# Depthwise taps on VectorE: the even tile of each pair runs one tap ahead of the odd one

## What is computed

```python
# x: (8, 256, 32, 32)
x = x + conv(layernorm_over_channels(x))
#   conv: qkv = 1x1 conv to 768 channels
#         agg = depthwise 5x5 conv of qkv (padding 2), then a grouped 1x1 conv
#         ms  = concat(qkv, agg);  per head of 24 channels: q, k = relu, v with a column of ones
#         out = q @ (k^T @ v);  out[..., :-1] / (out[..., -1:] + 1e-15)
#         out = 1x1 projection to 256 channels, then batchnorm
t = tokens(x)
t = t + ffn(layernorm(t))
#   ffn: softmax over 11 partitions from the image's mean token, top 2, weights of 6 experts;
#        gelu(t @ W1 + b1) per expert (341 wide), @ W2 + b2, weighted sum
x = from_tokens(t)
```

## Time and profile before

| what | value |
|---|---|
| median of 3 runs | 1441.13 us (1438.97 to 1443.95) |
| profiled execution | 1441.29 us, span 1439.6 us |
| PE busy | 1352.3 us (94%) |
| DVE busy | 1225.3 us (85%) |
| ACT busy | 1061.3 us (74%) |
| POOL busy | 977.9 us (68%) |
| mean granted clock of PE | 0.987 |

### The profile page before, as it was taken

The page is one execution under the profiler, slowest core; times in us unless marked ns, Lnnn a source line. Parts: engine busy times, 40 slices in busy tenths (PEclk is TensorE's granted clock), DMA queues, the critical chain, the costliest instruction groups (busy, mean ns, idle before and its releaser), DMA issues. The chain is left out here.

```text
span 1439.6 us, 18715 instructions
## 1 busy us (share of the span) xinstructions
PE 1352.3 (94%) x6844; PEld 771.3 (54%) x6844; DVE 1225.3 (85%) x1276; ACT 1061.3 (74%) x1890; POOL 977.9 (68%) x741
## 2 busy tenths in 40 slices
...
DMA packets 14251, 32.75 MB, mean 23 GB/s; under 512 B 2384, under 2 KB 5328, under 8 KB 13904
## 3 DMA queue, kind: packets, MB, share of 16 engines
...
## 5 line engine op out<-in xcount | busy, mean ns | idle before, releaser
L1154 DVE SCALAR_TENSOR_TENSOR dacc<-qkvs,dww,dacc 128x960 f32<-128x960 f32 (+4 forms) x930 | 1026.8, 1187 | 0.0
L1001 POOL TENSOR_TENSOR gl<-hb,gh 128x512 f16<-128x512 f32 x256 | 307.0, 1206 | 212.3 <-ACT hb L752 210.0
L962 POOL TENSOR_TENSOR dwo<-dwo,tapb 128x992 f32<-128x992 f32 (+2 forms) x100 | 231.9, 2319 | 85.7 <-ACT tapb L726 78.5
L855 ACT ACTIVATE hb<-wbk,b1s 128x512 f32<-128x512 f32 x256 | 174.1, 683 | 101.8 <-PE wbk L506 88.8
L521 PE MATMUL acc<-gh,w2h 128*128 128x512 f16 x512 | 194.6, 380 | 7.5 <-POOL gl L1001 5.7
L521 PE MATMUL acc<-gl,w2h 128*128 128x512 f16 x512 | 194.6, 380 | 0.0
L521 PE MATMUL acc<-gh,w2l 128*128 128x512 f16 x512 | 194.4, 380 | 0.0
L751 ACT ACTIVATE gh<-hb,ew 128x512 f16<-128x512 f32 x256 | 182.9, 714 | 3.0 <-PE acc L521 2.0
L752 ACT ACTIVATE hb<-hb,ew 128x512 f32<-128x512 f32 x256 | 182.3, 712 | 0.0
L506 PE MATMUL wbk<-th,w1h 128*128 128x512 f16 x512 | 152.6, 380 | 7.3 <-ACT kt L820 2.4
L506 PE MATMUL wbk<-tl,w1h 128*128 128x512 f16 x512 | 152.3, 379 | 0.0
...
## 6 DMA issues: line engine op xcount, KB each, us to landing
...
```

What stands on the lines that cost most here:

```text
L855: last = nc.scalar.activation(hb[:, f % GB, :], b[:], ACT.Gelu, bias=b1s[:, f % FT:f % FT + 1], scale=1.0 / (X_SCALE * W_SCALE))
L962: ins = nc.gpsimd.tensor_tensor(d3[:, oy, ox], d3[:, oy, ox], t3[:, iy, ix], ALU.add)
L1001: nc.gpsimd.tensor_tensor(gl[:, f % GB, :], hb[:, f % GB, :], gh[:, f % GB, :], ALU.subtract).then_inc(g_low, 1)
L1154: ins = nc.vector.scalar_tensor_tensor(out=dst[:, oy, ox], in0=i3[:, jy, jx], scalar=dww[:, m, tap:tap + 1], in1=a3[:, oy, ox], op0=ALU.mu ...
```

## The change

The order of the taps is now one list over all pairs and images. The even tiles' operations form one line, the odd tiles' another, and the list takes them in turn with the even line one ahead: first operation of the even line, second of the even line, first of the odd line, third of the even line, second of the odd line, and so on to the last of the odd line. The shift is not undone at the end of a pair or an image, so that the even tile of the next pair begins before the odd tile of this one has ended. Each operation still waits for the one two places ahead; at the two ends of the list, where two operations of one line follow each other, the wait is for the one just ahead. `taps_done` counts up to the odd tile's last operation in the new list. Places of small tasks are counted from the even tile's first operation of an image.

All five tables of words are new, and so are the places of the small tasks. The number of items of each kind is the same. Lines of after lie 11 to 15 below those of before (L1154 is L1169, L1143 is L1158, L1137 is L1152, L1051 is L1062, L962 is L973, L938 is L949, L922 is L933, L506 is L517, L521 is L532, L639 is L650, L648 is L659).

```diff
-def tap_ops(s):
-
-    return [(pair, tap, m) for pair in PAIRS for tap in tap_order(s, pair) for m in (2 * pair, 2 * pair + 1)]
+def tile_taps(side):
+
+    return [(s, tap, 2 * pair + side) for s in range(B) for pair in PAIRS for tap in tap_order(s, pair)]
+
+
+def tap_ops():
+
+    ahead, behind = tile_taps(0), tile_taps(1)
+    o = ahead[:1]
+    for a, b in zip(ahead[1:], behind):
+        o += [a, b]
+    return o + behind[-1:]
...
-tok.0.5 tok.0.6 tok.0.7 relu_q.0.0 kv.0.0.0 kv.0.0.1 low.1.0.1 mask.0.0 relu_q.0.1 att.0.0.0 b att.0.0.1
-att.0.0.2 att.0.0.3 scale.0.0.0 att.0.0.4 att.0.0.5 att.0.0.6 att.0.0.7 scale.0.0.1 back.0.0.0.0
...
+tok.0.7 relu_q.0.0 b kv.0.0.0 kv.0.0.1 mask.0.0 relu_q.0.1 att.0.0.0 att.0.0.1 att.0.0.2 att.0.0.3 b
+scale.0.0.0 att.0.0.4 att.0.0.5 att.0.0.6 low.1.0.1 att.0.0.7 squares.2.0.0 scale.0.0.1 back.0.0.0.0
...
-AGG_PLACES = {1: (14, 19, 71, 77), 2: (19, 20, 80, 84), 7: (17, 20, 74, 83), 8: (19, 21, 75, 83)}
-RAW_PLACES = {0: (81, 82), 1: (58, 65), 2: (67, 71), 7: (67, 69)}
+AGG_PLACES = {1: (14, 20, 73, 80), 2: (19, 21, 83, 86), 7: (15, 19, 74, 82), 8: (19, 21, 75, 83)}
+RAW_PLACES = {0: (82, 84), 1: (62, 65), 2: (66, 69), 7: (65, 70)}
...
-def taps_before(s, pair):
-
-    done = sum(len(tap_ops(i)) for i in range(s))
-    return done + sum(2 * len(tap_order(s, p)) for p in PAIRS[:PAIRS.index(pair)])
+TAPS_OF_ALL = tap_ops()
+
+
+def first_tap(s):
+
+    return TAPS_OF_ALL.index((s, CENTER, 2 * PAIRS[0]))
 
 
 def taps_done(s, pair):
 
-    return taps_before(s, pair) + 2 * len(tap_order(s, pair))
+    return TAPS_OF_ALL.index((s, None, 2 * pair + 1)) + 1
...
-                for n, (pair, tap, m) in enumerate(tap_ops(s)):
+                end = first_tap(s + 1) if s < B - 1 else len(TAPS_OF_ALL)
+                for no in range(first_tap(s), end):
+                    n = no - first_tap(s)
...
-                    if no > 1:
+                    if no in (1, len(TAPS_OF_ALL) - 1):
+                        dve.wait_ge(taps, no)
+                    elif no > 1:
 
                         dve.wait_ge(taps, no - 1)
```

More of the change, by code:

```diff
@@ L182 @@
-proj.-1.1.1 tok.0.6 tok.0.7 relu_q.0.0 kv.0.0.0 S F F squares.-1.1.0 squares.-1.1.1 sums.-1.1 b kv.0.0.1
-mask.0.0 relu_q.0.1 stats.-1.1 S b rnorm.-1.1 b att.0.0.0 att.0.0.1 att.0.0.2 G att.0.0.3 G rbc.-1.1.0 F
-rbc.-1.1.1 apply.-1.1.0 apply.-1.1.1 scale.0.0.0 att.0.0.4 att.0.0.5 att.0.0.6 high.-1.1.0 qkv.1.2.0
-qkv.1.2.1 att.0.0.7 G scale.0.0.1 G F qkv.1.3.0 S high.-1.1.1 low.-1.1.0 low.-1.1.1 G logits.-1 back.0.0.0.0
-back.0.0.0.1 back.0.0.1.0 qkv.1.3.1 back.0.0.1.1 F S S S F S squares.2.0.0 exp.-1 agg.0.2.0 agg.0.2.1 F
@@ new lines @@
+att.0.0.6 att.0.0.7 scale.0.0.1 back.0.0.0.0 back.0.0.0.1 qkv.1.3.0 high.-1.1.1 low.-1.1.0 S low.-1.1.1 S S
+back.0.0.1.0 G qkv.1.3.1 logits.-1 F F back.0.0.1.1 squares.2.0.0 exp.-1 agg.0.2.0 agg.0.2.1 agg.0.3.0 F
+squares.2.0.1 agg.0.3.1 sums.2.0 G S S F b S stats.2.0 G G G F S G F G S F S F rnorm.2.0 S b F agg.0.4.0
+rbc.2.0.0 G agg.0.4.1 F F rbc.2.0.1 agg.0.5.0 b G G b F S apply.2.0.0 G S b agg.0.5.1 G F kv.0.1.0 S F F
+qkv.1.4.0 F S apply.2.0.1 G G S G F S b G F S G S F b F G qkv.1.4.1 qkv.1.5.0 qkv.1.5.1 b F G S b F G S F G
@@ L199 @@
-mask.0.0 relu_q.0.1 b stats.-1.1 att.0.0.0 att.0.0.1 rnorm.-1.1 G S att.0.0.2 att.0.0.3 rbc.-1.1.0
-rbc.-1.1.1 apply.-1.1.0 apply.-1.1.1 G scale.0.0.0 F att.0.0.4 att.0.0.5 att.0.0.6 att.0.0.7 G qkv.1.2.0
-qkv.1.2.1 high.-1.1.0 high.-1.1.1 scale.0.0.1 F qkv.1.3.0 low.-1.1.0 low.-1.1.1 S logits.-1 back.0.0.0.0
-qkv.1.3.1 back.0.0.0.1 S b back.0.0.1.0 back.0.0.1.1 agg.0.2.0 G F F squares.2.0.0 agg.0.2.1 agg.0.3.0 S
-squares.2.0.1 sums.2.0 exp.-1 agg.0.3.1 G F S b stats.2.0 G F F rnorm.2.0 S G G S G S F F b G S G F b S F S
@@ L204 @@
-agg.0.4.0 G rbc.2.0.0 G S agg.0.4.1 F S b rbc.2.0.1 G agg.0.5.0 apply.2.0.0 S apply.2.0.1 b b agg.0.5.1 F S
-G F F qkv.1.4.0 G S G F F F F G S F S b G qkv.1.4.1 qkv.1.5.0 G S G qkv.1.5.1 b b F S S G G kv.0.1.0 S F b F
-G F S S G kv.0.1.1 S mask.0.1 b
+F S agg.-1.0.0 agg.-1.0.1 G agg.-1.1.0 agg.-1.1.1 S att.-1.1.0 att.-1.1.1 att.-1.1.2 G qkv.0.0.0 att.-1.1.3
+S b scale.-1.1.0 att.-1.1.4 att.-1.1.5 att.-1.1.6 att.-1.1.7 F scale.-1.1.1 F b F F qkv.0.0.1 qkv.0.1.0 G
+qkv.0.1.1 S back.-1.1.0.0 back.-1.1.0.1 high.1.0.0 low.1.0.0 back.-1.1.1.0 S G b back.-1.1.1.1 high.1.0.1
@@ L221 @@
+F att.0.0.4 S att.0.0.5 att.0.0.6 att.0.0.7 scale.0.0.1 b back.0.0.0.0 F G high.-1.1.0 high.-1.1.1
+low.-1.1.0 low.-1.1.1 S b F S logits.-1 back.0.0.0.1 back.0.0.1.0 G G back.0.0.1.1 agg.0.2.0 b S G exp.-1
+agg.0.2.1 F S agg.0.3.0 agg.0.3.1 G F F G S F G S F G S b F S G b S agg.0.4.0 G F F S F S agg.0.4.1 F G
+agg.0.5.0 S b F agg.0.5.1 G F S G S G G kv.0.1.0 F S F F S G S S G G kv.0.1.1 mask.0.1 G S b F b F G S b b F
+G S b G S F S G F
 """.split()
 END = """
-G F S agg.-1.0.0 agg.-1.0.1 agg.-1.1.0 agg.-1.1.1 G F att.-1.1.0 att.-1.1.1 att.-1.1.2 att.-1.1.3
```

89 lines of the change are left out of this document (45 added, 44 removed).

## The result

The changed kernel is slower by a hair: 1444.72 us in the median of 20 runs against 1443.93 of the kernel before, a ratio of 1.0017 with a 95% interval of 1.001 to 1.0025, or some 2.4 us. 1438.8 was forecast, so the sign was wrong. Single executions of both kernels are spread over 4 to 6 us (those of before lie near 1439, 1441.4 and 1444), and the median of before falls into the uppermost of its three groups, so the two medians are closer (1.0005) than the means (1.0015). They are more than the 2.4 of the ratio: each trace is one execution, and where the others lose or win isn't shown.

A forecast was written before the change was run, and what follows sets the result against it. PE was taken to bound the middle images and a chain through ACT, POOL and DVE the head. Terms -2.0 + 2.5 - 2.5 - 0.5 = -2.5 took 1441.3 to 1438.8 us, range 1431.5 to 1447.

The forecast's parts named there:

- sign of being wrong: Wrong if a middle image is more than 1 us shorter, or if the first ffn comes later than before.
- What bounds the kernel: PE sets the pace in middle images, DVE follows with 4.6 us to spare; in the head an ACT, POOL, DVE chain.
- DVE's wait would shrink to 1 us: Middle images: DVE's 3.3 us of waits before the two reciprocals should shrink to about 1.
- The head, -2.0: 36 to 250 us: first reciprocal 6.2 us earlier, second scaling ends 2.1 ahead; -2.0 us, range -5 to +4.
- from there image 1's chain keeps the lead: After image 0's second scaling, image 1's chain is one of PE and ACT and keeps the 2.1 us lead.
- The rule that I set aside: Two-SBUF-input DVE and GpSimd operations exclude each other; about 1.2 us more in the head, total 1440.0; not adopted.
- Images 1 to 6, +2.5: Two more bank handshakes per image, about 0.5 us, times five: +2.5 us, range -2 to +5.
- Image 7, -2.5: Last image: both PE waits of 0.9 go, att wait loses 0.7; -2.5 us, range -4 to +2.
- The tail, -0.5: One ffn in the rbc wait saves 1.3, a split between att evictions costs 0.8; -0.5 us, range -2 to +1.
- DVE did not set the pace: Rival: DVE sets the pace, so 3.3 us per image come back in five images; about 1420 us, chance 0.10.
- The clock did not help: Rival: shorter head waits keep PE's clock up in two of five half-rate stretches; 1434.1 us, chance 0.14.
- The slower rival: Late base tap and low half on POOL's chain, first reciprocal after about 131.5; head +6.5, 1447.3 us, chance 0.14.

The follow-up runs named there:

- with one input: Centre taps read one SBUF tensor, base left out of the sum; ratios to the kernel before: changed kernel 0.9986 (1438.98 us), kernel before 0.9988.
- the alternating kernel with the same tables: Alternating taps of the kernel before with all tables and places of the changed kernel; 0.9995 of the kernel before.
- the mended table: Changed kernel with two words moved in the table of images 2 to 6; 0.9991 of the kernel before, 1440.84 us.

## Why the prediction was wrong

In the traces the changed kernel ends 3.8 us behind where 2.5 ahead was forecast. Of these 6.3 us, 3.5 lie in the head and image 1 (2.0 ahead was forecast, 1.5 behind measured at the last agg of image 2), 2.1 in image 7 and 1.1 in the tail; the middle images lost 0.4 less than forecast. The collisions explain the loss against before, but the gain would not have come without them either: with one input the changed kernel has 0.9986 and before 0.9988. Neither sign of being wrong that the prediction names came true: the middle image grew by 0.5 us, and the first ffn came earlier.

**What bounds the kernel** held: the middle image is PE's, and with DVE's waits almost as before (3.5 us for den in four pieces, 0.8 at the routing step) nothing depends on them. PE's waits there are eight in place of seven:

```profile
PE wbk L607 <- ACT sum_b L851: 0.3, 1, 0.3
...
PE wbk L633 <- ACT qkvs L816: 0.2, 1, 0.2
```

```profile
DVE den L1062 <- ACT den L845: 3.5, 4, 1.6
DVE rt L1077 <- ACT rt L791: 0.8, 1, 0.8
```

That DVE's wait would shrink to 1 us was wrong.

**The head, -2.0.** Up to the second scaling the steps were right in kind and cautious in size: the first reciprocal came 8.25 us earlier (6.2 taken), the odd centre tap waited 2.04 (2.0 worked out), the second scaling ended at 135.56, 4.2 ahead of 139.75 (2.1 taken). The step that failed is the sentence that from there image 1's chain keeps the lead. The first ffn was 0.5 us ahead, and the last agg of image 1 was 1.8 late. The one-input kernels show what took it: collisions of centre taps with POOL, about 1 us each, in image 0 (1.25 for a step of the mask, 3.11 for the low half) and image 1 (3.30 for a base addition ahead of the mask). Behind the late mask of image 1 the clock adds to it. PE's att there, after and with one input:

```profile
226.89 3.84 PE L626 MATMUL wbk<-kvm,qr 128*128 128x144 f32 x16 [2.65 <-issue]
```

```profile
223.98 2.54 PE L626 MATMUL wbk<-kvm,qr 128*128 128x144 f32 x16 [1.66 <-issue]
```

PE waited 2.65 us in place of 1.66, and the same sixteen products then took 3.84 us in place of 2.54: the granted clock is 0.50 (half rate, 1.2 GHz) from 226.8 to 230.2 after, and 1.00 from 222 to 230 with one input. Here, then, the collision cost 1.0 us itself and 1.3 through the clock. After, the stretches at half rate that answer are 121.0 to 124.4, 131.3 to 141.5, 172.2 to 182.5, 226.8 to 230.2 and 237.1 to 240.5:

```profile
sum 30.70, PE 24.89 PEld 21.76 DVE 25.33 ACT 12.81 POOL 19.59; mean PE 4.98 PEld 4.35 DVE 5.07 ACT 2.56 POOL 3.92
```

They hold 30.7 us, all of them in the head; the fourth begins at the att that waited for the mask. Before's five hold 27.3, one of them in the tail, but the earlier trace rows leave out a sixth:

```profile
44.30:47.70 3.40, 3.40 (x4) 1.48 (x5) 3.40 (x4) 3.40 (x10) 2.99 (x1) 0.50 0.00 0
```

With it before has 30.7 us too, 27.3 of them in the head. So the change moved the half rate and did not add to it over the whole. And DVE ran late into image 1's second half: its reciprocal stands at 346.65, where the alternating kernel with the same tables has it at 342.71, though the two were level at a reciprocal of 189.7 (189.9). On the way DVE lost 1.3 us at the centre tap of 220.64, waited 0.7 at the reciprocal of 241.18, and lost 2.1 at a small step of the routing that adds two tensors of SBUF and takes 0.17 us in the alternating kernel. It started 0.06 us behind POOL's addition of squares and ended with it:

```profile
260.60 2.35 POOL L908 TENSOR_TENSOR nrm<-nrm 128x1024 f32<-128x1024 f32 x1 [9.94 <-ACT nrm L776]
```

```profile
260.66 2.31 DVE L1093 TENSOR_TENSOR wsel<-wsel 128x11 f32<-128x11 f32 x1
```

POOL's scaling ahead of a split product waits for the late reciprocal, and PE for the split product:

```profile
347.67 1.97 POOL L949 TENSOR_TENSOR kt<-kt,den 128x1024 f32<-128x1024 f32 x1 [3.20 <-DVE den L1062]
...
356.12 0.39 PE L532 MATMUL acc<-gh,w2h 128*128 128x512 f16 x1 [1.15 <-POOL gl L1012]
```

The kernel with alternating taps has no such wait there; before has one of 1.5, so this one is a loss against the alternating kernel and not against before. Beyond the place at 226.89, how much of the head's loss is the clock's and how much the collisions' own can't be parted by these runs.

**The rule that I set aside** was the step behind this. The row at 134.81 (a centre tap of 1.21 us beside a scaling) was read as evidence against a whole block, and the rule was priced at one collision, 1.2 us, in image 0. But that row agrees with the rule: the centre tap came first and POOL second, and POOL's run of two took 4.78 in place of 4.0. The Trainium skill, SBUF — State Buffer, section SBUF: two separate sides, calls the port pair an exclusive lock that a DVE operation with two SBUF inputs and a GpSimd operation hold for the whole instruction. The traces bear it out on both sides: 2.91 and 2.60 us for centre taps that came second, 3.43, 3.30 and 3.11 for POOL's operations that did, and 1.28 and 2.31 once the second input is gone. I should have gone through each centre tap's new place for what POOL has there and who waits for it.

**Images 1 to 6, +2.5.** Right in mechanism and nearly in size: from image 2 to image 6 the lag grew by 2.1 us, and the mended table gave 3.6 back in its trace.

**Image 7, -2.5.** Mis-sized: -0.4. The two waits of 0.9 went, and others came in their place, of which none was looked for:

```profile
PE wbk L626 <- ACT qr L785: 1.3, 1, 1.3
PE acc L532 <- POOL gl L1012: 1.1, 2, 0.6
PE wbk L614 <- ACT vt L838: 0.8, 1, 0.8
PE wbk L599 <- ACT hb L866: 0.8, 1, 0.8
```

I read it so that an ffn that fills one wait is missing at another; no run puts one back there.

**The tail, -0.5.** +0.6. The wait at rbc fell from 3.06 to 1.76, as worked out; but without an ffn ahead of the first att of the second half PE waits there three times (0.78, 0.27 and 0.69), where before it waited once (0.69), and the logits, which waited for nothing before, wait 1.15 for th. For all of this 0.8 was taken:

```profile
1289.92 1.22 PE L626 MATMUL wbk<-kvm,qr 128*128 128x144 f32 x8 [0.78 <-ACT qr L829]
1291.41 1.25 PE L626 MATMUL wbk<-kvm,qr 128*128 128x144 f32 x8 [0.27 <-ACT den L845]
1293.35 0.76 PE L626 MATMUL wbk<-kvm,qr 128*128 128x144 f32 x4 [0.69 <-ACT den L845]
...
1331.80 1.06 PE L659 MATMUL wbk<-ident,sv 128*128 128x128 f32 x8 [1.76 <-POOL sv L922]
...
1339.61 0.58 PE L663 MATMUL wbk<-rws,us 128*128 128x11 f32 x4 [1.15 <-ACT th L747]
```

**The rivals.** DVE did not set the pace. The clock did not help: 30.7 us at half rate in both. The slower rival named POOL's chain in image 0 as its place and a first reciprocal after 131.5 as its point; the reciprocal came at 125.69, so it is refuted as put, though the loss did come over POOL.
